# One GpSimd product of 128x2048 with a repeated row in place of four of 128x512, in a selective-scan block on one core

## What is computed

```python
x_branch, z = jnp.split(x @ W_in, 2, axis=-1)          # 1024 channels each
xc = silu(causal_conv(x_branch, conv_w, 4 taps) + conv_b)
ssm = xc @ W_x                                         # B, C: 16 states each; dt
dt = softplus(ssm[..., -1:] + dt_bias);  A = -exp(A_log)
def step(h, inp):
    xt, dtt, Bt, Ct = inp
    h = h * exp(dtt[:, :, None] * A[None]) + (dtt * xt)[:, :, None] * Bt[:, None, :]
    return h, einsum('bds,bs->bd', h, Ct)
y = (scan of step over the tokens + xc * D_param) * silu(z)
out = y @ W_out
```

## Time and profile before

| | |
|---|---|
| runs | 6000.39, 6002.64, 6003.43 us; median 6002.64 |
| profiled execution, span | 6003.3 us, within the runs |
| DVE busy | 5250.3 us (87%) |
| PE busy | 4882.5 us (81%), granted clock 0.952 on average |
| POOL busy | 3613.3 us (60%) |
| ACT busy | 2899.3 us (48%) |
| DMA | 327 MB, 55 GB/s |
| product v (L883, POOL) | 2048 of 1273 ns |
| scan (L1072, DVE) | 2048 of 1270 ns |
| addition to acc (L1085, DVE) | 2048 of 723 ns |

### The profile page before, as it was taken

The page is one execution under the profiler, slowest core; times in us unless marked ns, Lnnn a source line. Parts: engine busy times, 40 slices in busy tenths (PEclk is TensorE's granted clock), DMA queues, the critical chain, the costliest instruction groups (busy, mean ns, idle before and its releaser), DMA issues.

```text
span 6003.3 us, 80311 instructions
## 1 busy us (share of the span) xinstructions
PE 4882.5 (81%) x21508; PEld 3165.1 (53%) x21508; DVE 5250.3 (87%) x6743; ACT 2899.3 (48%) x4931; POOL 3613.3 (60%) x2815
## 2 busy tenths in 40 slices
PE   2999999999987777777777777877777787787767
PEld 1788888888863444444444444444444444444444
DVE  9666666666654999999999999999999999999998
ACT  1111111111115666675666666666675666656654
POOL 5233333333323777777777767777777777767785
PEclk9999999999998899999999999999999999999978
DMA  2111111111111112111121211212111121211111
GB/s 61 41 41 42 42 42 42 42 42 42 42 54 63 54 55 73 53 53 57 60 66 54 70 52 59 65 57 70 53 53 57 59 66 54 70 51 61 55 60 50
DMA packets 192158, 327.26 MB, mean 55 GB/s; under 512 B 24032, under 2 KB 56800, under 8 KB 187632
## 3 DMA queue, kind: packets, MB, share of 16 engines
q1 hardware_dynamic: 191728, 322.51, 17.2%
HBM read 254.25 MB, written 68.19 MB: 54 GB/s over the span
## 4 chain that ended last, share of the span: by engine, by line
DVE 32%; issue 16%; PE 13%; POOL 4%; ACT 3%; DVEq 2%; DMA 1%; SPq 0%; ACTq 0%; POOLq 0%
DVE hs L1072 18%; DVE acc L1085 11%; PE ht L1192 5%; POOL v L883 3%; PE mm L1181 3%; PE mm L1133 2%; DVEq L763 2%; PE mm L1141 1%; ACT decay L1013 1%; DVE xc L1044 1%; DVE rtb L1061 1%; PE mm L1156 1%; PE mm L1149 1%; PE mm L1173 0%; POOL dt L896 0%
## 5 line engine op out<-in xcount | busy, mean ns | idle before, releaser
L883 POOL TENSOR_TENSOR v<-u,b_rep 128x512 f32<-128x512 f32 x2048 | 2563.1, 1273 | 916.2 <-DVE hs L1072 627.2
L1072 DVE TENSOR_TENSOR_SCAN hs<-decay,carry,v 128x512 f32<-128x512 f32 x2048 | 2599.8, 1270 | 78.1 <-POOL v L883 36.4
L1192 PEld LDWEIGHTS ht<-ident,hs 128*128 128x128 f32 x8192 | 1020.4, 149 | 1968.7 <-issue 1291.4
L1192 PE MATMUL ht<-ident,hs 128*128 128x128 f32 x8192 | 1363.4, 293 | 760.3 <-DVE hs L1072 528.5
L1013 ACT ACTIVATE decay<-dt,a_neg 128x512 f32<-128x512 f32 x2048 | 1387.6, 685 | 985.3 <-DVE hs L1072 972.5
L1085 DVE SCALAR_TENSOR_TENSOR acc<-ht,c_now,acc 128x512 f32<-128x512 f32 x2048 | 1480.6, 723 | 38.8 <-PE ht L1192 37.3
L469 ACT ACTIVATE sg<-gate 128x512 f32<-128x512 f32 (+1 forms) x192 | 108.0, 562 | 1331.8 <-PE up L515 1331.8
L1133 PE MATMUL mm<-x_in,w_in 128*128 128x512 f32 x1024 | 553.1, 638 | 92.4 <-DVE xc L1044 50.0
L1181 PE MATMUL mm<-w_out,yt 128*128 128x512 f32 x1024 | 553.6, 639 | 53.8 <-DVE xc L1044 35.1
L1149 PE MATMUL mm<-w_in,x_z 128*128 128x512 f32 x1024 | 539.8, 618 | 0.0
L105 POOL TENSOR_TENSOR h<-h,h_small 128x1408 f32<-128x1408 f32 x64 | 166.2, 2597 | 439.9 <-DVE h_small L99 439.9
(11 more groups left out here) (129 smaller groups left out, 6906.9 us busy)
## 6 DMA issues: line engine op xcount, KB each, us to landing
b_rep<-ssm_d SPq DMA_DIRECT2D x512, 256.0 KB, 3.8
rtb<-res_d SPq DMA_DIRECT2D x128, 256.0 KB, 3.0
xt<-in_L_attn_x SPq DMA_DIRECT2D x64, 256.0 KB, 2.8
xnt_d<-xntb SPq DMA_DIRECT2D x64, 256.0 KB, 2.7
rt<-in_L_attn_x SPq DMA_DIRECT2D x64, 256.0 KB, 2.6
res_d<-rt SPq DMA_DIRECT2D x64, 256.0 KB, 2.0
x_in<-xnt_d SPq DMA_DIRECT2D x16, 1024.0 KB, 4.8
x_z<-xnt_d SPq DMA_DIRECT2D x16, 1024.0 KB, 4.9
```

The lines of the kernel that those rows point to most:

```text
L883: nc.gpsimd.tensor_tensor(v[k % 2][:, j, :], u[g][:, j, :], b_rep[k % 4][:, :], ALU.mult).then_inc(v_ready, 1)
L1072: nc.vector.tensor_tensor_scan(h[k % 2][:, j, :], decay[n % 4][:, :], v[k % 2][:, j, :], carry[:, s, GD * g + j:GD * g + j + 1], ALU.mult, ...
L1192: last = nc.tensor.transpose(ht[n % 2][:, j, :], h[k % 2][:, j, t * P:(t + 1) * P], ident[:, :])
```

## The change

POOL's four products of a slot become one. Its second operand is the same row of B for all four blocks, given as an access pattern in which the dimension of the blocks has stride zero. Its waits are those of all four blocks: before, block j waited for scan j of slot k-2, now the whole waits for the fourth scan. The instruction raises v_ready by four at its end.

```diff
         def drive(c, k):
 
             g = k // NS
-            for j in range(GD):
-                if j == 0:
-                    wait(pool, b_loaded[k % 4], c.at(128, 16 * (k // 4) + 16))
-                if k % NS == 0:
-                    wait(pool, u_ready, c.at(8, 4 * g + j + 1))
-                wait(pool, scanned, c.at(128, 4 * (k - 2) + j + 1))
-                nc.gpsimd.tensor_tensor(v[k % 2][:, j, :], u[g][:, j, :], b_rep[k % 4][:, :], ALU.mult).then_inc(v_ready, 1)
+            wait(pool, b_loaded[k % 4], c.at(128, 16 * (k // 4) + 16))
+            if k % NS == 0:
+                wait(pool, u_ready, c.at(8, 4 * g + 4))
+            wait(pool, scanned, c.at(128, 4 * (k - 2) + 4))
+            nc.gpsimd.tensor_tensor(v[k % 2][:, :, :], u[g][:, :, :],
+                                    b_rep[k % 4][:, :].unsqueeze(1).broadcast_to([P, GD, CL]),
+                                    ALU.mult).then_inc(v_ready, GD)
```

## The result

The changed kernel takes 6085.07 us in the median of four runs (6079.35 to 6085.69) against 6001.95 before (also four runs): a ratio of 1.0138, 95% interval 1.0124 to 1.0153, or 83 us more. Forecast were 6122 us, within 6040 to 6190. The mechanism is the one forecast; some 36 us of its size are not.

What follows compares the result with a forecast made beforehand. DVE was taken to bound phase B without holes; its small-operation waits rise from 44.6 to 158.4 us (+113.8), plus 1.5 and 3.3 us for late products: +119 us on the 6002.64 median, 6122 us, range 6040 to 6190.

Steps and rivals of the forecast that it cites:

- The hold lasts for the whole instruction: Small DVE operations in phase B wait until the running GpSimd instruction, all 2048 elements, ends; waits 158.4 instead of 44.6 us.
- The rival of a hand-over after each row of 512: Port is handed to DVE after each 512 elements of the long product: 6042 us, chance 0.07.
- The product's length: POOL's merged product v takes 4.54 us, with bounds 3.69 and 5.09.
- GpSimd stays in time: Product v is ready for DVE's scans, except k=12, 1.5 us in all, and the very first, 3.3 us.
- The sign of being wrong: In the profile after, halo and c_now stay as they are, or DVE waits for v by more than 20 us.
- DVE has no holes there: In phase B, scans and additions to acc fill 4080.4 of 4113 us, so any DVE wait lengthens the kernel equally.
- The places: Where DVE's small operations meet the long product in a chunk: c_now after scan n=3, conv at n=34, 54, 60, 72.
- n=54: Conv at n=54: halo waits 0.63 us for the product's end, 15 times, 9.5 us; the copy is free.
- n=60 and 72: Convs at n=60 and n=72: halo comes 2.97 us after the product's start, waits 1.57 us; 47.1 us in all.
- halo at n=34: Conv at n=34: the product ends at 2991.82, halo comes at 2990.29 and waits 1.53 us, 15 times.
- the copy then falls behind the small dt product: Conv at n=34: after halo's wait, the copy to xb waits 1.15 us for POOL's next product, 15 times.
- places where DVE's lost time is taken out of the waits it has anyway for PE: DVE's existing waits for PE absorb some loss; a little kept back, slower put at 0.89 instead of 0.92.

Runs made afterwards that it cites:

- the replacements: Changed kernel with c_now and the copy to xb as TENSOR_REDUCE, halo as SCALAR_TENSOR_TENSOR with a PSUM operand: 5975.63 us, ratio 0.9960.
- the coarse wait and four of 512: Changed kernel with its one wait per slot kept, but four products of 128x512 instead of one: 5996.67 us, ratio 0.9993 to the kernel before.
- two of 1024: Changed kernel with its one wait per slot kept, but two products of 128x1024 instead of one: 6069.88 us, ratio 1.0119.
- the three and the four replacements: c_now, xb copy and halo in other forms, or keep too: changed kernel 5975.63 and 5980.36 us; kernel before 5991.61 and 5986.85 us.
- c_now's alone: Changed kernel with only the c_now copy made a TENSOR_REDUCE over an axis of length one: 6040.74 us, ratio 1.0070.

## Why the prediction was right, and where its size was off

- **The hold lasts for the whole instruction.** Right, and shown three ways: by the ends of halo and c_now in the trace, by c_now at 0.745, 1.836 and 3.727 us with products of 512, 1024 and 2048, and by the replacements that take the waits away beside the same product. The rival of a hand-over after each row of 512 falls with c_now: it would have ended within 1.1 us. This is also what the Trainium skill says (SBUF — State Buffer, "SBUF: two separate sides"), and the trace agrees: 0.02 to 0.03 us after the product's end, halo has ended too. One thing was missed: a hold can also outlast the instruction that runs, when POOL's next one goes first (the keep of 5.77 us above).
- **The product's length.** 4.54 forecast, 4.537 measured; the halved one 2.36 forecast, 2.360 measured. The fixed part of 0.185 us taken from two widths of another product carried over. The 4.497 us of the Trainium skill (GPSIMD Engine Reference, "Elementwise — side-by-side cycle accounting") is 0.04 short here.
- **GpSimd stays in time.** Right: 2.8 us for the first product (3.3 forecast), 1.8 us at n=48 (1.5 forecast), nothing else of size. The sign of being wrong, DVE waiting for v by more than 20 us, has to be read as new waiting: 36.4 of the 40.4 us were there before.
- **"DVE has no holes there"** was a misreading, though the premise built on it held nearly in full. The 4080.4 us of scans and additions add up durations that overlap: the scan shown above at 2945.45 ends at 2946.72, and the addition behind it starts at 2946.64. DVE was in fact idle for 107 us between the first scan and the end, and for 98 with the change: idle time can take back part of a new wait, and 10 of the 83 us went that way.
- **The places.** c_now 61.6 us forecast, 56.5 measured; n=54 9.5 and 9.5; n=60 and 72 47.1 and 43.2 (30 x (1.66 - 0.22)); halo at n=34 23.0 and 18.5. The common fault, which n=54 shares and hides by chance: I took the time from issue to the product's end as loss, but part of the operation's own time runs under that wait. The loss is that time less some 0.13 us for halo and 0.09 for c_now, not that time in full. In c_now one of the 16 also escaped: in the first chunk, which has no additions between its first scans, it was not held (0.17 us).
- **The step that failed most: "the copy then falls behind the small dt product"**, 1.15 us x 15 = 17.3 us. It never did. Whenever a halo had waited in the changed kernel, the copy behind it came through in 0.15 us, though in 14 cases POOL's next product started within 0.1 us of halo's end. I had taken the blocked copies of the trace before for the rule. Counted over phase B of the kernel before, they are 5 of 25 such cases; with the coarse wait and four of 512, 3 of 44; with two of 1024, 0 of 14. What decides those few is open: the start times of copy and product do not sort them.
- **Not foreseen: 9 us back at the loop's edge.** Before the chunks' first scans DVE idled 41.6 us before and 32.7 after, without the first product's wait. I had kept back "places where DVE's lost time is taken out of the waits it has anyway for PE", which gave 3.5.

Of the difference of 31 us in new waits, 17 are the copy, 9 the overlap and the escape, 4 to 5 halo at n=34. The rest is the 12 us of idle time that came back at the loop's edge and before the additions to acc, against which the profiled execution has 5 us of later start of phase B.

## What to carry to other kernels

Before merging GpSimd instructions, list the small COPY and TENSOR_SCALAR operations on DVE that read and write SBUF, and compare their mean with their shortest time: if they already wait for the end of a GpSimd instruction, as here, a longer one makes each meeting longer. In this kernel, bound by DVE, GpSimd's saving of 241 us was worth nothing by itself, and such side effects decided. The repair was on DVE's side: the same copy as a TENSOR_REDUCE over an axis of length one, or another operand from PSUM, or two steps later in the order. But count what comes back at the loop's edge and in the waits for PE before trusting the sum of the waits removed; the best kernel of this study, 5975.63 us (0.9960 of before), has the long product and those replacements.

## What the runs showed of the hardware that was not expected

- An operation of three numbers is held like one of 1408: halo, 128x3, up to 1.97 us, as is c_now with 64 up to 4.06.
- When a held halo ends and POOL's next product starts, the copy behind halo mostly gets through all the same: 89 of 97 cases in four traces. It is no rule, and it does not bound the wait: one keep of two numbers was held 5.77 us, past the ends of five products of 1.27 us.
- TENSOR_REDUCE with an axis of length one copies 128x64 in 0.218 us (COPY 0.168 to 0.194 unhindered) and 128x3 in 0.148 (0.155); a SCALAR_TENSOR_TENSOR that passes over a PSUM operand takes 0.207 us for 128x3 (0.220). In the kernels that have them (six for c_now, five for the other two) none was held: the longest took 0.222, 0.160 and 0.219 us.
- At the loop's edge DVE idles about 3.5 us before the first scan of a pass in the kernel before, and about 2.7 in the changed one (41.6 and 32.7 us, twelve passes). With one wait to a slot the edge is 8 to 14 us cheaper in each row of the table above, whatever the product's length, and the three and the four replacements make it dearer (c_now's alone does not: 36.9 us). That DVE's pause depends on POOL's code, and on where its own small operations stand, was not expected, and its cause was not tested.
